# Context keys and values of the first head projected ahead of the norm's turn, packed heads and placed projections in an eight-layer transformer kernel

## The reference, cut to what matters

```python
x = x + L0_xattn(layernorm(x), ctx)   # 32 query heads of 128, 8 key/value heads, keys from ctx alone, rotary
x = x + L0_ffn(layernorm(x))          # silu(x @ w1 + b1) * (x @ w2 + b2) @ w3 + b3
x = x + L1_xattn(layernorm(x), ctx)   # 16 query heads of 96, 4 key/value heads, keys from [ctx, layernorm(x)]
x = x + L1_ffn(layernorm(x))          # base GEMM + 8 low-rank experts weighted by sparsemax
x = x + L2_xattn(layernorm(x), ctx)   # 32 query heads of 128, 4 key/value heads, keys from [ctx, layernorm(x)]
x = x + L2_ffn(layernorm(x))          # top-16 router over 64 low-rank experts
x = x + L3_xattn(layernorm(x), ctx)
x = x + L3_ffn(layernorm(x))
```

## Time and profile before

| | us |
|---|---|
| three runs | 2202.68, 2204.60, 2206.17 |
| median | 2204.6 |
| the profiled execution | 2207.11 |
| its span, first to last instruction | 2205.3 |

### The profile page before, as it was taken

The page is one execution under the profiler, slowest core; times in us unless marked ns, Lnnn a source line. Parts: engine busy times, 40 slices in busy tenths (PEclk is TensorE's granted clock), DMA queues, the critical chain, the costliest instruction groups (busy, mean ns, idle before and its releaser), DMA issues.

```text
span 2205.3 us, 32364 instructions
## 1 busy us (share of the span) xinstructions
PE 2012.5 (91%) x11920; PEld 1698.5 (77%) x11920; DVE 1491.8 (68%) x2990; ACT 1148.9 (52%) x2347; POOL 833.3 (38%) x821
## 2 busy tenths in 40 slices
PE   4999999999689999977899999999987899987886
PEld 3788888888568888866789889889876678765753
DVE  3777778777646555556566666666665487876898
ACT  2666666666115555441556555555551287874433
POOL 5645555453522222043431231321135531443562
PEclk9999999999889999998999999999999999987998
DMA  3101110110101010001101010010011100211210
GB/s 144 37 31 49 48 49 30 48 39 20 65 27 32 15 37 25 1 30 58 39 20 39 30 49 20 20 39 20 22 39 51 51 13 20 78 58 63 77 39 19
DMA packets 20571, 87.61 MB, mean 40 GB/s; under 512 B 3264, under 2 KB 9152, under 8 KB 11968
## 3 DMA queue, kind: packets, MB, share of 16 engines
q1 hardware_dynamic: 20416, 85.55, 11.0%
HBM read 84.49 MB, written 1.05 MB: 39 GB/s over the span
## 4 chain that ended last, share of the span: by engine, by line
PE 75%; DVE 10%; issue 6%; POOL 6%; ACT 2%; DMA 1%; SPq 0%; POOLq 0%; DVEq 0%; ACTq 0%
PE ps_s L304 10%; PE ps_s L306 9%; PE ps_s L305 9%; PE ps_t L699 7%; PE ps_t L304 6%; PE ps_t L306 6%; PE ps_t L305 6%; PE ps_o L304 4%; PE ps_o L306 4%; PE ps_o L305 4%; PE ps_o L1405 3%; PE ps_t L1441 2%; PE ps_s L1391 2%; DVE xn L358 1%; POOL wo_lo L330 1%
## 5 line engine op out<-in xcount | busy, mean ns | idle before, releaser
L747 ACT ACTIVATE l_pt_hi<-ps_t 128x512 fp32r<-128x512 f32 (+1 forms) x512 | 244.2, 515 | 336.6 <-PE ps_t L699 336.2
L806 DVE TENSOR_REDUCE nmax<-ps_s 128x1 f32<-128x768 f32 x192 | 183.7, 957 | 304.5 <-PE ps_s L306 303.5
L814 DVE TENSOR_TENSOR l_pt_lo<-ps_t,l_pt_hi 128x512 fp32r<-128x512 f32 (+1 forms) x512 | 281.4, 580 | 7.3 <-ACT l_pt_hi L747 7.3
L699 PE MATMUL ps_t<-ident,l_p 128*128 128x128 f32 x1664 | 236.9, 274 | 29.9 <-DVE l_pt_lo L814 24.2
L774 ACT ACTIVATE l_p<-ps_s,nmax 128x768 f32<-128x768 f32 x192 | 173.5, 903 | 160.9 <-DVE nmax L806 160.3
L699 PEld LDWEIGHTS ps_t<-ident,l_p 128*128 128x128 f32 x1664 | 198.0, 140 | 73.3 <-issue 32.9
L328 POOL TENSOR_TENSOR wq_hi<-raw_big,one 128x512 fp32r<-128x512 f32 (+1 forms) x108 | 118.0, 1093 | 331.4 <-PE ps_t L306 312.3
L304 PE MATMUL ps_o<-l_pt_hi,l_v_hi 128*128 128x256 f32 (+1 forms) x832 | 237.2, 285 | 3.2 <-DVE l_pt_lo L814 3.1
L306 PE MATMUL ps_o<-l_pt_hi,l_v_lo 128*128 128x256 f32 (+1 forms) x832 | 235.0, 283 | 0.0
L305 PE MATMUL ps_o<-l_pt_lo,l_v_hi 128*128 128x256 f32 (+1 forms) x832 | 234.9, 282 | 0.0
L328 POOL TENSOR_TENSOR wo_hi<-raw_big,one 128x512 fp32r<-128x512 f32 (+2 forms) x100 | 107.2, 1072 | 326.8 <-PE ps_t L306 319.4
(11 more groups left out here) (370 smaller groups left out, 5477.7 us busy)
## 6 DMA issues: line engine op xcount, KB each, us to landing
raw_big<-in_l_wq SPq DMA_DIRECT2D x18, 1024.0 KB, 4.8
raw_big<-in_l_wo SPq DMA_DIRECT2D x18, 1024.0 KB, 4.8
raw_big<-in_f_w SPq DMA_DIRECT2D x7, 1024.0 KB, 5.0
raw_kv<-in_l_wkv SPq DMA_DIRECT2D x12, 512.0 KB, 5.7
raw_f<-in_f_w SPq DMA_DIRECT2D x4, 1024.0 KB, 4.8
q_nat<-in_f_w2n SPq DMA_DIRECT2D x4, 1024.0 KB, 5.2
q_nat<-in_f_w1n SPq DMA_DIRECT2D x4, 1024.0 KB, 4.9
raw_big<-in_l_wq SPq DMA_DIRECT2D x4, 768.0 KB, 4.8
```

Of the source, the lines that this page charges most:

```text
L699: mm = e.transpose(o[:, kk * P:(kk + 1) * P], sp.p[:, k % 3, at:at + P], ident[:, :])
L747: e.activation(sp.pt[u % 2][0][:, k0:k0 + nk, qt * P:(qt + 1) * P], ps_t[p % 2][:, 0:nk * P].rearrange("p (k q) -> p k q", q=P), ACT.Copy) ...
L806: e.tensor_reduce(nmax[:, i:i + 1], self.scores_out(k), AX.X, ALU.max, negate=True).then_inc(s_max, 1)
L814: e.tensor_tensor(pt[1], ps_t[p % 2][:, 0:nk * P].rearrange("p (k q) -> p k q", q=P), pt[0].bitcast(F32), ALU.subtract).then_inc(s_tlo, 1)
```

## The change

It has these parts.

1. **Ahead.** In the second and third attention, k0, v0, k1 and v1 of the first key/value head are taken out of the job list. TensorE does them (`ahead_pe`, 48 matmuls) right after the last GEMM of the feed-forward layer before, ahead of the norm's turn; the values are copied, turned by four transposes per batch (`turn_ahead`) and split.
2. **Packed heads** in the second attention. The Q weights are loaded so that each of three Q jobs yields 96 rows of its own head and 32 rows of the fourth head; six DMAs from SBUF to SBUF assemble the fourth head, and after attention six per batch spread its output into the free rows of the other three. Four Q jobs become three, an O job has three parts instead of four, and the heads are used in the order 0, 1, 3, 2.
3. **Placed projections.** Jobs of first and last groups, and all of the second attention, have slots written out.
4. **Start.** Loads, splits and the context are ordered by batch; job k0 runs before x is turned.
5. **GpSimd waits for xn** in every norm but the first. f0's last GEMM does three quarters of its contraction for all tokens first, into the turn banks; f2's last GEMM waits per tile.

```diff
@@ FIRST, MIDDLE, LAST
-            "l1": ["k1 K1 o0 v1 V1 o1 o2 o3 q0 k0 K0 q1 v0 V0 q2 q3"],
-        FIRST = {"l0": "k0 v0 q0 q1 q2 q3", "l1": "q0 k0 K0 q1 v0 V0 q2 q3", "l2": "q0 k0 K0 q1 v0 V0 q2 q3"}
+        FIRST = {
+            "l0": "k0@-6 v0@-5 q0@-4 q1@-3 q2@-2 q3@-1 k1@0 v1@2,3,3,4 "
+                  "q0@8 k0@9,9,10,10 q1@10,10,11,11 v0@12 q2@13,13,14,14 q3@14,14,15,15",
+            "l1": "q0@-3 K0@-2 q1@-1 q2@0 V0@1 K1@4 V1@6 "
+                  "q0@8 K0@9 q1@10 V0@11 q2@12 k0@13,13,14,14 v0@14,14,15,15",
+            "l2": "q0@-3 K0@-2 q1@-1 q2@0 V0@1 q3@2 K1@4 V1@6 "
+                  "q0@8 q1@10 q2@12 q3@14",
+        }
+        MIDDLE = {
+            "l1": "k1@0 K1@1 o0@2 o1@3 v1@4 V1@5 o2@6 o3@7 q0@8 K0@9 q1@10 V0@11 q2@12 k0@13,13,14,14 v0@14,14,15,15",
+        }
+        LAST = {
+            "l0": "k1@0 o0@2 o1@4 v1@5 o2@7 o3@9 o0@14,14,15,15 o1@16,16,17,17",
+            "l1": "k1@0 K1@2 V1@2 v1@4 o0@5 o1@7 o2@9 o3@10 o0@14 o1@16",
+            "l2": "o0@1 o1@3 o2@6 o3@9 o0@13 o1@15",
+        }
@@ Norm
             def dve(self, e, link):
...
+                if self.i == 0:
+                    split_context(e, 0)
                 e.wait_ge(s_rstd, self.i + 1)
...
             def pool(self, e):
                 e.wait_ge(s_ve, self.i + 1)
                 e.tensor_tensor(rstd[:, :], veps[:, :], mhalf[:, :], ALU.pow).then_inc(s_rstd, 1)
+                if self.i:
+                    e.wait_ge(s_xn, TT * (self.i + 1))
@@ packed loads and moves
+        def load_packed_q(sp, src, before):
+            sp.wait_ge(w_rdy[before[0]], before[1] * 8)
+            to = raw_big[:, :, 0:384].rearrange("p d (t c) -> p d t c", c=P)
+            for t in range(3):
+                sp.dma_start(to[:, :, t, 0:96], src[:, :, t * 96:(t + 1) * 96]).then_inc(s_pq, 16)
+                sp.dma_start(to[:, :, t, 96:P], src[:, :, 288 + 32 * t:320 + 32 * t])\
+                    .then_inc(w_in["q"] if t == 2 else s_pq, 16)
+            def move_queries(self, e, g):
+                q = self.s.q[g % 2]
+                for t in range(3):
+                    e.wait_ge(g_free, self.full(self.find["q", g, t, False]))
+                    for a in q:
+                        e.dma_start(a[32 * t:32 * t + 32, 3, :].bitcast(F32), a[96:P, t, :].bitcast(F32)).then_inc(s_qmove, 16)
+            def move_out(self, e, g, b):
+                cols = slice(b * SQ, (b + 1) * SQ)
+                e.wait_ge(s_qmove, 96 * (g + 1))
+                e.wait_ge(s_olo, self.c.unit + g * UNITS + b * HG + 3)
+                for a in self.s.q[g % 2]:
+                    for t in range(3):
+                        e.dma_start(a[96:P, t, cols].bitcast(F32), a[32 * t:32 * t + 32, 3, cols].bitcast(F32)).then_inc(s_omove[b], 16)
+            def sp_packed(self, e):
+                l, c = self.l, self.c
+                for g in range(l.groups):
+                    if g + 1 < l.groups:
+                        load_packed_q(e, self.wq[g + 1], self.raw_before(g))
+                        load(e, "kv", None, self.wkv[g + 1], ("kv", c.kv + g + 1), cols=2 * l.hd)
+                    self.move_queries(e, g)
+                    if g:
+                        self.move_out(e, g - 1, 1)
+                    load_packed_o(e, self.wo[g], ("q", c.q + g + 2) if g + 1 < l.groups else self.raw_before(g))
+                    self.move_out(e, g, 0)
@@ ahead
+            def ahead_pe(self, e):
+                hd, end = self.l.hd, self.c.g - 8
+                e.wait_ge(w_rdy["kv"], 8 * (self.c.kv + 1))
+                for n, (b, c0) in enumerate(((0, 0), (0, hd), (1, 0), (1, hd))):
+                    e.wait_ge(g_free, end + (n + 1 if self.tail_in_ring else 0))
+                    o = self.ahead_bank(n)
+                    for d in range(DK):
+                        mm = passes(e, o[0:hd, :], planes(W["kv"], slice(None), d, slice(c0, c0 + hd)),
+                                    planes(cT, slice(None), d, slice(b * SK, (b + 1) * SK)), d == 0, d == DK - 1)
+                    mm.then_inc(s_af, 1)
@@ f0_pe
-            e.wait_ge(s_f0lo, 4)
-            token_gemm(e, 8, c0, lambda k, t: planes(f_h, slice(None), k, slice(t * P, (t + 1) * P)),
-                       lambda k: planes(W["f"], slice(None), k, slice(None)), range(4))
+            for ks in (range(3), range(3, 4)):
+                for t in range(TT):
+                    for k in ks:
+                        if t == 0:
+                            e.wait_ge(s_f0lo, k + 1)
+                        mm = passes(e, turn_banks[t][:, :], planes(f_h, slice(None), k, slice(t * P, (t + 1) * P)),
+                                    planes(W["f"], slice(None), k, slice(None)), k == 0, k == 3)
@@ start, on SP and GpSimd
             e.dma_start(x[:, :, :], A["x"]).then_inc(s_x, 16)
+            load(e, "kv", a0.c.kv, a0.wkv[0], None, cols=256)
+            e.dma_start(craw[:, :, 0:SK], A["ctxT"][:, :, 0:SK]).then_inc(s_ctx[0], 16)
             e.dma_start(ident[:, :], A["ident"]).then_inc(s_const, 16)
             load(e, "q", a0.c.q, a0.wq[0], None)
-            e.dma_start(craw[:, :, :], A["ctxT"]).then_inc(s_ctx, 16)
-            load(e, "kv", a0.c.kv, a0.wkv[0], None, cols=256)
+            e.dma_start(craw[:, :, SK:C], A["ctxT"][:, :, SK:C]).then_inc(s_ctx[1], 16)
...
+            for piece in range(2):
+                split(e, "kv", a0.c.kv, None, piece, cols=256)
             norms[0].pool(e)
+            for piece in range(2, 4):
+                split(e, "kv", a0.c.kv, None, piece, cols=256)
             split_all(e, "q", a0.c.q, None)
...
+            split_context(e, 1)
@@ TensorE's program
             e.wait_ge(s_const, 16)
-            norms[0].pe(e)
-            a0.pe(e)
+            a0.pe(e, norms[0].pe)
             norms[1].pe(e)
             f0_pe(e)
+            a1.ahead_pe(e)
+            a1.turn_ahead(e, 0)
             norms[2].pe(e)
+            a1.turn_ahead(e, 1)
             a1.pe(e)
```

More of the change, by code:

```diff
@@ L55, in __init__ @@
         self.scale = float(hd) ** -0.5
+        self.packed = hd == 96
+        self.ahead = self_keys
+        self.qt = 3 if self.packed else HG
+        self.rows = P if self.packed else hd
 L0 = Layer("l0", 8, 128, False, 1, True)
@@ L452, in job, with listed @@
                         self.values.setdefault((j.end + 2) | 1, []).append(j)
[L453 to L457, removed]
+                n = self.N
+                def listed(text, g):
+                    seen = set()
+                    for item in text.split():
+                        name, at = item.split("@")
+                        kv = g // l.kv_every
+                        if g == 0:
+                            again = name in seen or (l.ahead and name[0] in "kv")
+                            own = 0 if not again else {"q": 1}.get(name[0], kv + 1)
+                        elif g < l.groups - 1:
+                            own = {"q": g + 1, "o": g - 1}.get(name[0], kv + (name[1] == "0"))
+                        else:
+                            own = {"o": g - 1 if name not in seen else g}.get(name[0], kv)
+                        seen.add(name)
+                        at = [int(a) for a in at.split(",")]
+                        at = at * (l.qt if name[0] == "o" else DK) if len(at) == 1 else at
+                        job(name, own, [g * TILES + a for a in at])
+                self.begin = int(FIRST[l.name].split()[0].split("@")[1])
+                listed(FIRST[l.name], 0)
+                for g in range(1, l.groups - 1):
+                    if l.name in MIDDLE:
+                        listed(MIDDLE[l.name], g)
+                        continue
                     order = ORDER[l.name][g % l.kv_every].split()
@@ L461, in place @@
                     kv = g // l.kv_every
-                    for n, name in enumerate(order):
+                    for m, name in enumerate(order):
                         own = {"q": g + 1, "o": g - 1}.get(name[0], kv + (name[1] == "0"))
[L464 to L472, removed]
+                        if own < (l.groups if name[0] in "qo" else self.kvs):
+                            job(name, own, [g * TILES + (4 * m + part) // pair * 2 + ((4 * m + part) % pair >= even)
+                                            for part in range(4)])
+                listed(LAST[l.name], l.groups - 1)
+                end = [n + 3, n + 3, n + 4] if l.packed else [n + 2, n + 2, n + 2, n + 4]
+                job("o2", l.groups - 1, end)
+                job("o3", l.groups - 1, end)
                 self.slots = range(self.begin, n + 7)
@@ L575, in next_q @@
                     if g + 1 < l.groups:
-                        split(e, "q", c.q + g + 1, self.full(self.find["q", g, 3, False]), piece, cols=HG * l.hd)
+                        if l.packed and piece == 0:
+                            e.wait_ge(s_pq, 80 * (g + 2))
+                        split(e, "q", c.q + g + 1, self.full(self.find["q", g, l.qt - 1, False]), piece, cols=HG * l.hd)
```

(3 more changed lines are left out.)

230 lines of the change are left out of this document (180 added, 50 removed).

## The result

| | us |
|---|---|
| before, beside it on the same chip | 2203.6 (2200.8 to 2206.2, 4 runs) |
| after | 2131.75 (2128.8 to 2137.8, 4 runs) |
| ratio | 0.968, 95% interval 0.965 to 0.970 |
| predicted | 2122, range 2106 to 2148 |

What follows compares the result with a forecast made beforehand. TensorE, working 2012.5 of 2205.3 us, was taken as the bound, with 193 us of idling to fill. Terms summed to -82.3 from the profiled 2207.1, giving 2124.8, or 2122.3 on the median's scale; range 2106 to 2148.

Steps and rivals of the forecast that it cites:

- Start, -17: Start up to the first scores: reordered loads and splits bring the scores earlier, -17 us, bounds -10 and -19.
- GpSimd splits K/V in 5.5 us: Start: GpSimd's K/V weight splits, with rstd of 1 us between, let the first context matmul begin at 13.4.
- f0, second norm: f0's last GEMM runs 36 matmuls (8.2 us) under VectorE's fourth quarter; q0 earlier by 7 us, bounds -4 and -8.
- rival 2: Second norm: late packed weights hold GpSimd before rstd, q0 at 633, 2135 us in all; chance 0.07.
- Second attention: Fewer jobs before scores -14, group 0 -5, two middle groups -12.2, last group with tail -5; sum -36.2 us.
- Moves: Fourth-head DMAs in the second attention priced at nothing inside groups; at the tail zero, bounds 0 and +3 us.
- 4.8 us after its output: Second attention's tail: second spread, six issues of 0.43 and 2 us landing, ends before ps_o and last attend's 6.
- Norm's turn at the fast rate: Both norms with ahead matmuls: the turn's twelve transposes take 1.53 us, not 2.82 as after idling.
- Third attention's last group, +2 to +3: Last group of the third attention gets O jobs in odd slots, costing +2 to +3 us.
- GpSimd waits for xn, -6.8: Norm before f2 -3.3, last norm -3.0, f2's last GEMM -1.8, before last attention +1.3; bounds -2 and -9 us.
- The split starts 2 us later: +1.3: Before the last attention TensorE already waits for wq_lo; the delayed split costs +1.3 us, bounds 0 and +4.
- Rival 5: Whole kernel gains more than the sum, as less idling spares cold matmuls; about 2108 us, chance 0.09.

Runs made afterwards that it cites:

- start experiment: Changed kernel with VectorE's split of the first context half held back until GpSimd has split the K/V weights; 2139.3 us in one execution.

## Why the prediction was right, and where its terms were off

The mechanism held. Up to the third attention's first scores, where 74.6 of the 76.3 us are won, no term is off by more than 1.6; behind them every small term but one (xn before f2) misses by 1 to 3.5, and most of it upwards. The measured 2131.75 lies 9.5 above the forecast's 2122.3: 6.0 is the miss of the sum in span, and the rest is how the profiled executions stand to their medians (2.5 over it assumed, 0.9 under it found).

- **Start, -17 against -15.4.** Data were there as worked out: GpSimd began on the K/V weights at 7.00. The step "GpSimd splits K/V in 5.5 us" took a duration from a row with VectorE idle. Beside VectorE's context split three of its splits took 1.05 and the first matmul came at 14.85 instead of 13.4. Scores came at 39.60 instead of 37.2. Only 0.9 of these 2.4 lie before q0 (27.07 against 26.2); 1.5 lie behind it, where the sum had four Q jobs in 11.0 us and they took 12.5: the four transposes of the values stand between them, and the third waited 0.73 us for VectorE's rotation of the first.
- **f0, second norm.** -7.4 against -7, and undoing the order alone gave 7.1 to 7.7 of the 8.2 back. Late packed weights (rival 2) never showed: rstd ran at 598.27, well before the 618 that would have been the sign.
- **Second attention.** The three jobs in front, group 0, and the middle groups "near 79" (78.38) came as worked out, and the last group's -5 as well. But its reason was coarse: packing gave 0.9 there (at most 2.5, as said above), the placement of the other jobs the rest.
- **Moves.** Zero inside the groups was right, with 64 KB pieces landing in 2.0 and 2.5 us and 32 KB pieces in 1.8, under 34 us of slack. At the tail "4.8 us after its output" used 0.43 us an issue; three issues took 1.8, so 1.70 us of wait showed. The packed Q loads landed in 3.0 us (192 KB) and 2.7 (64 KB), where the packets under 512 B rose from 3264 to 17104. That such runs miss line rate, as the Trainium skill says (DMA: Bandwidth & Descriptors, Specifications), may be; here no engine waited for them in a middle group.
- **Norm's turn at the fast rate.** 1.48 and 1.47 us behind the ahead matmuls, 2.82 without them. The Trainium skill (TensorE: Matmul & The Clock Gate, Part 4: PE-mode transpose) has the full clock not engage for transposes; the runs decide against that here.
- **Third attention's last group, +2 to +3 against +5.1.** The term that was mis-sized is the price of O jobs in odd slots: five of its six stand there, and moving four of them to even slots took 7.7 back, 1.9 each. Group 0's -4.7 against -3 hid 1.7 of this miss in the sum, by luck.
- **GpSimd waits for xn, -6.8 against nothing.** The largest miss, and the part whose mechanism was wrong. The term for xn was right at every norm (1.92 us), the term for what the later splits delay was not. "The split starts 2 us later: +1.3" was 2.0. f2's last GEMM waited 0.90 for wq_lo where it had waited 1.93 for f_h_lo, and the stretch before it grew by 0.9, so -1.8 became nothing. And the last norm's -3.0 left out what the last layer, whose first wo split starts at 1944.61 behind xn, gives back: 1.6 to 2.5.

```profile
1634.52 0.47 PE L316 MATMUL ps_s<-wf_hi,f_h_hi 128*128 128x512 f32 x1 [0.90 <-POOL wq_lo L356]
```

- Rival 5, more than the sum since less idling spares slow matmuls, is seen in single places (the turns) and in the 6.9 us of TensorE's busy time that no removed matmul explains. It did not carry the sum, which fell short of the forecast.
- **Range.** The lower ends of the terms' bounds add to -44 with the moves' +3, which is 2160; the prediction's -41 and 2164 don't come out of them. Nothing hangs on it, since its 2148 was set apart from them.

Open: 1.0 us of loss in the last layer beyond the wait, and the later stages of the start experiment. The 0.9 of gain in the last attention beyond xn is less than that stage scatters (272.1 to 274.0 over the runs with the wait at the last norm). The start's new order as a whole, the first attention's placement and f2's wait per tile were undone by no run; for them the timelines speak alone.

## What to carry to other kernels

Cut a pipelined stage at its slots and find which of them wait while they hold no job; work belongs there, and work taken out of a stage pays only where no wait takes its place (packing: 6.6 us and more in a full group, at most 2.5 in one with gaps). A wait that frees an engine for its neighbour is priced at both ends: what the neighbour wins, and who waits next for the engine that stood still. A duration read where a neighbouring engine was idle may be too short once the change makes them work side by side.

## What the runs showed of the hardware

**VectorE and GpSimd slow each other unequally.** xn beside GpSimd's splits takes 5.26 us for four operations that take 1.92 alone, 1.3 for each, about as long as one split (1.04 to 1.34), while GpSimd's eight splits take 9.9 us whether xn runs beside them or not. At the start it is the other way about: GpSimd's 128x256 splits rise from 0.61 and 0.72 to 1.05 beside VectorE's subtractions from SBUF. The Trainium skill (SBUF — State Buffer, Who interferes with whom) calls the shared port pair an exclusive lock; steps of about one whole instruction per xn operation agree.

**Idle time can cost twice.** A wait of 1.70 us left the granted clock at 1.00, one of 6.24 and one of 7.92 us were followed by 0.50, that is 1.2 instead of 2.4 GHz. In the last case 3 us held 14 matmuls instead of 25. The length of the last wait doesn't decide alone: waits of 3.08 and then 2.13 us were followed by 0.50 too, and the turn behind a wait of 3.1 us took 1.53 us in one run and 2.50 in another.

**Issue cost of moves.** A DMA within SBUF took 0.5 to 0.75 us to issue on SP, against the 0.43 I had used.
